# A fused patch-embedding, attention and expert kernel: attention as one stream of 128 steps, taken in pairs on TensorE

## The reference, cut to what matters

```python
h = tok_ref(x, W, b, cls_token, pos_enc)         # 32 images, 36 patches + 1 class token, 256 wide
h = concatenate([h, txt], axis=1)                # + 77 text tokens: T = 114 tokens an image
h = h + attn_ref(layernorm(h), Wq, Wk, Wv, Wo)   # 16 heads of 64, causal softmax, + its own input
h = h + ffn_ref(layernorm(h), ...)               # 8 experts, top 2, capacity 570, exact gelu
# attn_ref: q, k, v = x @ Wq, x @ Wk, x @ Wv
#   scores = q k^T / 8 + causal mask;  out = softmax(scores) v;  x + out @ Wo
```

## Time and profile before

| | us |
|---|---|
| median of 3 runs | 954.19 (951.41 to 954.93) |
| the profiled execution | 953.52 |
| its span, first to last instruction | 951.6 |
| first score matmul / last output projection's end | 51.8 / 679 |
| busy: PE, PEld | 869.6 (91%), 754.2 (79%) |
| busy: DVE, ACT, POOL | 556.2 (58%), 516.0 (54%), 370.5 (39%) |
| mean granted clock of TensorE | 0.96 |

### The profile page before, as it was taken

One profiled execution on the slowest core, in us unless ns is written; L12 is line 12 of the kernel. 1 busy time (PEld: TensorE's weight loads), 2 busy tenths in 40 slices (PEclk: granted clock), 3 DMA queues, 4 the chain that ended last, 5 costly groups with the idle time before them and its releaser, 6 DMA issues.

```text
span 951.6 us, 19817 instructions
## 1 busy us (share of the span) xinstructions
PE 869.6 (91%) x6897; PEld 754.2 (79%) x6897; DVE 556.2 (58%) x2433; ACT 516.0 (54%) x1686; POOL 370.5 (39%) x677
## 2 busy tenths in 40 slices
PE   4898999999999999999999999997708999999996
PEld 4676787797788778779777877875708999999996
DVE  3566347528645753863775485476236767777761
ACT  3368438807824961880684386186016555565551
POOL 2134225345425424543542653554430333322333
PEclk8799899999999999999999999998758999999999
DMA  8224302012002101200200200100135655444322
GB/s 252 50 58 132 98 13 60 2 41 74 1 8 65 43 1 42 71 2 22 68 16 1 59 9 2 38 2 1 24 100 179 158 117 134 102 121 121 83 26 25
DMA packets 61908, 57.64 MB, mean 61 GB/s; under 512 B 26784, under 2 KB 56652, under 8 KB 61697
## 3 DMA queue, kind: packets, MB, share of 16 engines
q1 hardware_dynamic: 41170, 45.15, 15.5%
q0 software_dynamic: 18944, 9.76, 6.5%
q10 hardware_dynamic: 1696, 1.49, 0.6%
HBM read 34.25 MB, written 21.89 MB: 59 GB/s over the span
## 4 chain that ended last, share of the span: by engine, by line
PE 82%; DVE 4%; POOL 4%; issue 4%; ACT 3%; DMA 1%; SPq 1%; POOLq 0%; DVEq 0%; ACTq 0%
PE bank L380 14%; PE bank L382 13%; PE bank L381 13%; PE pT_bank L1241 6%; PE score_bank L1232 6%; PE o_bank L1252 6%; PE score_bank L1130 4%; POOL pr L573 2%; PE o_bank L381 2%; PE o_bank L382 2%; PE o_bank L380 2%; PE score_bank L380 2%; PE score_bank L381 2%; PE score_bank L382 2%; ACT pr L706 2%
## 5 line engine op out<-in xcount | busy, mean ns | idle before, releaser
L573 POOL TENSOR_SCALAR pr<-pr,rc 114x114 f32<-114x114 f32 x512 | 179.7, 371 | 233.7 <-DVE rc L991 233.7
L706 ACT ACTIVATE pr<-sm,nb 114x114 f32<-114x114 f32 x512 | 192.1, 379 | 22.6 <-DVE nb L987 21.2
L983 DVE CUSTOM_DVE_ANT_0 sm<-score_bank,mask 114x114 f32<-114x114 f32 x512 | 110.5, 272 | 55.2 <-PE score_bank L1232 55.2
L604 POOL DMA_INDIRECT out_dram<-yout,dest x40 | 74.0, 1849 | 163.0 <-ACT yout L758 161.5
L554 POOL DMA_INDIRECT slots_dram<-rows,slot x64 | 72.8, 1137 | 128.2 <-DVE slot L950 93.3
L624 ACT ACTIVATE kT<-bank 128x456 f32<-128x456 f32 x64 | 34.1, 532 | 146.8 <-PE bank L382 146.8
L380 PE MATMUL bank<-xT_hi,wqkv_hi 128*128 128x456 f32 x256 | 103.5, 404 | 0.0
L1232 PEld LDWEIGHTS score_bank<-kT,qT 64*114 64x114 f32 x1024 | 62.1, 177 | 45.5 <-issue 35.3
L706 ACT ACTIVATION_READ_ACCUMULATOR pr<-sm,nb 114x1 f32 x512 | 97.0, 189 | 0.0
L381 PE MATMUL bank<-xT_lo,wqkv_hi 128*128 128x456 f32 x256 | 94.3, 368 | 0.0
L382 PE MATMUL bank<-xT_hi,wqkv_lo 128*128 128x456 f32 x256 | 94.3, 368 | 0.0
(11 more groups left out here) (198 smaller groups left out, 2228.1 us busy)
## 6 DMA issues: line engine op xcount, KB each, us to landing
stage_a<-in_L_ffn_w_dram SPq DMA_DIRECT2D x8, 1024.0 KB, 5.0
stage_b<-in_L_ffn_w_dram SPq DMA_DIRECT2D x8, 1024.0 KB, 7.1
slots_dram<-fill SPq DMA_DIRECT2D x8, 605.6 KB
xs<-slots_dram SPq DMA_DIRECT2D x8, 605.6 KB
pix<-in_x_dram SPq DMA_DIRECT2D x96, 36.0 KB, 2.3
hraw<-in_txt_dram SPq DMA_DIRECT2D x8, 308.0 KB
out_dram<-h SPq DMA_DIRECT2D x8, 308.0 KB
pix<-pix SPq DMA_DIRECT2D x7, 216.0 KB, 2.6
```

Source lines behind the costliest of these rows:

```text
L573: p = pool.tensor_scalar(pr[:, m % 4, i, :], pr[:, m % 4, i, :], rc[:, m % 4, i:i + 1], 1.0, ALU.mult, ALU.mult)
L604: pool.indirect_dma_start(out, bass.IndirectOffsetOnAxis(ap=dest[e % 2][:, t:t + 1], axis=0), yout[:, t, :], None, compute_op=ALU.add).the ...
L706: a = act.activation(pr[:, n % 4, i, :], sm[:, n % 2, i, :], ACT.Exp, bias=nb[:, n % 2, i:i + 1], scale=SCALE, accum_out=rs[:, n % 4, i:i ...
L983: m = dve.tensor_tensor_reduce(sm[:, n % 2, i, :], score_bank[i % 2][0:T, i // 2 * T:(i // 2 + 1) * T], mask[:, :], 1.0, NEG, ALU.add, ALU ...
```

## The change

1. The groups' loops become one loop over N = 0 to 132 (`steps()`: 128 steps and five that drain), g and n = divmod(N, 16). Nothing drains at a group's end.
2. On TensorE an even step issues `scores` of N and N + 1, then `weigh_values` of N - 5 and N - 4. Each step issues its own transposes, of N - 3 (`LAG_T` = 3, `LAG_O` = 5). `score_bank` now holds both steps, in other columns. VectorE masks N and N + 1 in the even step, the reciprocal and the low half between them.
3. The output projection of group g - 1 stands in steps 4 and 5 of group g (`AT_O`); the embedding in step 9 in one of the three banks instead of `score_bank[0]`; the second halves of the values in steps 5 to 8 of their own group; the first halves in steps 14, 15 and 0.
4. `pack` moves from step 10 to step 4 (`AT_PACK`), the addition into hx to steps 1 and 2, into two buffers. Dispatches go one by one into steps 4 to 11 of two groups later; other small parts get other steps.
5. The prologue makes four value projections instead of eight, and K, Q, K instead of Q, K, Q.

```diff
+        LAG_T, LAG_O = 3, 5
+        AT_O, AT_V2, AT_E, AT_M, AT_Y, AT_L, AT_X = 4, 5, 6, 9, 10, 11, 13
+        AT_PACK, AT_RSTD1, AT_RSTD2 = 4, 10, 8
+        STATS2, MOMENTS2, NORM2 = {6: (0, 1), 7: (2, 3)}, 7, {9: (0, 1, 2, 3)}
+        STATS1, MOMENTS1, NORM1 = {8: (0, 1), 9: (2, 3)}, 9, {11: (0, 1), 12: (2, 3)}
+        AT_DISPATCH = 4
+        def chunk_at(g, n):
+            name, c = ("Q", (n + 2) // 2) if n % 2 == 0 else ("K", (n + 3) // 2)
+            return (name, HP * g + c) if HP * g + c < HP * G else None
+        def value_jobs(g, n):
+            if n == 0 and g > 0:
+                return [(g, 3)]
+            if g + 1 < G:
+                return {14: [(g + 1, 0)], 15: [(g + 1, 1), (g + 1, 2)]}.get(n, [])
+            return []
...
 # TensorE
-                m = pe.matmul(score_bank[h][0:T, b * T:(b + 1) * T], qT[head, c % 2, tokens], kT[head, c % 2, tokens], start=True, stop=True)
+                m = pe.matmul(score_bank[h][0:T, tokens], qT[head, c % 2, tokens], kT[head, c % 2, tokens], start=True, stop=True)
+            for N, g, n in steps():
+                if n == AT_X and g + 1 < G:
+                    transpose_tokens("X", g + 1, xn, xn_done)
+                if n % 2 == 0:
+                    for m in (N, N + 1):
+                        if m < STEPS:
+                            scores(m)
+                    for m in (N - LAG_O, N - LAG_O + 1):
+                        if 0 <= m < STEPS:
+                            weigh_values(m)
+                if LAG_T <= N < STEPS + LAG_T:
+                    transpose_probs(N - LAG_T)
+                if g < G:
+                    if chunk_at(g, n):
+                        project(*chunk_at(g, n))
+                    for f, b in value_jobs(g, n):
+                        project_v(f, b, 0)
+                    if n - AT_V2 in range(GB):
+                        project_v(g, n - AT_V2, 1)
+                    if n == AT_E and g + 1 < G:
+                        transpose_patches(g + 1)
+                    if n == AT_M and g + 2 < G:
+                        embed(g + 2)
+                    if g > 0:
...
+                        if n - AT_O in range(2):
+                            project_o(g - 1, n - AT_O)
 # VectorE, in a step N
+                if N < STEPS and N % 2 == 0:
+                    mask_scores(N)
+                if 1 <= N <= STEPS:
+                    dve.wait_ge(exp_done, N)
+                    dve.reciprocal(rc[:, (N - 1) % 4, :], rs[:, (N - 1) % 4, :]).then_inc(recip_done, 1)
+                if N >= LAG_O:
+                    give_low_outputs(N - LAG_O)
+                if N < STEPS and N % 2 == 0:
+                    mask_scores(N + 1)
 # ScalarE, in a step N
+                if N >= LAG_O:
+                    take_outputs(N - LAG_O)
+                if LAG_T <= N < STEPS + LAG_T:
+                    m = N - LAG_T
+                    act.wait_ge(pT_done, m + 1)
+                    act.activation(pT[:, m % 2, :, :], ...).then_inc(pT_copied, 1)
+                if N < STEPS:
...
+                if g + 2 < G and n == AT_PACK:
+                    pack(g + 2)
 # GpSimd, in a step N
+                if g < G and n in (1, 2):
+                    if n == 1:
+                        pool.wait_ge(xn_done, GB * (g + 1))
...
+                    pool.tensor_tensor(hx[g % 2][:, b, :], hraw[:, b, :], xn[:, b, :], ALU.add).then_inc(hx_done, 1)
+                if 1 < g < G and n - AT_DISPATCH in range(TOPK * GB):
+                    dispatch(g - 2, n - AT_DISPATCH)
 # SP
+            for g in range(G):
+                if g + 1 < G:
                     sp.wait_ge(hx_done, 2 * g + 2)
                     load_text(g + 1)
+                if g + 2 < G:
                     sp.wait_ge(packed, g + 2)
                     load_pixels(g + 2)
```

More of the change, by code:

```diff
@@ L296, in count @@
+        JOB_AT = {job[:2]: i for i, job in enumerate(JOBS)}
         def count(jobs, engine=None):
             return sum(1 for j in jobs if engine is None or engine in j[2])
[L299 to L343, removed]
@@ L369, in ebank_free, with steps @@
             return [{"H": (gelu_done, NF * f + n + 1), "S": (xs_done, NX * f + n + 1), "Y": (y_done, CT * f + n + 1)}[was]]
-        def pair(g, n):
-            return g * PAIRS + n
+        STEPS = PAIRS * G
+        def steps():
+            for N in range(STEPS + LAG_O):
+                yield (N,) + divmod(N, PAIRS)
         def wait_all(eng, waits):
@@ L596, in _ @@
+            for i in range(TOPK * GB):
+                dispatch(G - 2, i)
             rstd(G - 1, vareps2, rstd2_done, ve2, rstd2)
@@ L1039, in _ @@
-            body(0, first=True)
-            for g in range(1, G - 2):
-                body(g)
-            body(G - 2)
-            body(G - 1, last=True)
-            jobs = Jobs("end")
+                            drain_e(g + 1, i)
+                    if n == AT_M + 1 and g + 2 < G:
+                        drain_embedded(g + 2)
+                    if g > 0:
+                        if n == AT_Y + 1:
+                            drain_y(g - 1)
+                        if n == AT_L + 1:
+                            route(g - 1, 0)
+                        if n - 1 - AT_O in range(2):
+                            drain_o(g - 1, n - 1 - AT_O)
@@ L1308, in body @@
-                if not last and not (isinstance(g, int) and g == G - 2):
-                    embed(g + 2)
-                if not first:
-                    count_places(jobs, g - 1)
-                if first:
-                    pe.wait_ge(wo_lo_done, 1)
-                pe.wait_ge(o_lo, pair(g, PAIRS))
-                for k in range(2):
-                    project_o(jobs, k)
-                if not last:
-                    project(jobs, "Q", 0)
-                    project(jobs, "K", 0)
-                    project(jobs, "Q", 1)
@@ L1322, in _ @@
[L1322 to L1332 removed]
+                            logits(g - 1)
+                        if n - AT_O in range(2):
+                            project_o(g - 1, n - AT_O)
@@ L1335, in e_claim @@
+                if n == AT_C and g > 1:
+                    count_places(g - 2)
+            for i in range(2):
+                project_o(G - 1, i)
+            transpose_tokens("Y", G - 1, rows[(G - 1) % 2], xn2_done)
+            logits(G - 1)
+            count_places(G - 1)
             def e_claim(name, e, k):
```

700 lines of the change are left out of this document (302 added, 398 removed).

## The result

The changed kernel takes **928.86 us** (median of 4 runs, 927.24 to 930.4), the kernel before 952.8 in the same comparison (951.38 to 954.93): a ratio of 0.9745, 95 % interval 0.9723 to 0.9766. The forecast was 921.8, with a range of 905 to 946. The profiled execution took 927.2 (span 925.3), so it is 5.4 over the forecast's own sum, which was made against a profiled execution too.

What follows compares the result with a forecast made beforehand. TensorE bounds the groups, through changes of the used array's shape, then seams. From the profiled 953.5 us, 34.1 less for pairs, 6.0 less for one stream and 8.4 more for the pixels make 921.8 us; range 905 to 946.

Steps and rivals of the forecast that it cites:

- What bounds the kernel: TensorE in the groups: mainly changes of the used array's shape, then 19.3 us of waits, nearly all near group seams.
- Rival 3: TensorE's gaps belong to each block's first operands, pairs bring them back: 955.9 us, no change; chance 0.06.
- Part 1: Scores and weighings issued for two steps at once on TensorE: 27 fewer shape changes a group, -34.1 us.
- Parts 1 and 2: Group loop: pairing two steps' scores and weighings, -34.1 us; one stream instead of draining and refilling groups, -6.0 us.
- part 3: Pixel packing moved to step 4: group 0's weighing in step 6 waits, +8.4 us once; hidden in steady groups.
- Step 13's size: TensorE's wait in step 13, 0.6 plus about 1.3 beyond its transposes: 1.9 us in each of seven groups, 13.3.
- One for one: Group 0's clock: the new wait brings a low-clock stretch, the one after the old 2.11 us idle goes: 0.
- Rival 2: The clock falls at step 13 of each group, 7 x 3.3 = 23 us: 945 us; chance 0.15.
- First scores: Start of the loop: four value projections leave the prologue, so scores start 5.6 us earlier; net nothing.
- Rival 4: ScalarE takes over in the pairs: slower than before from 5.87 us a pair, 966 at 6.0; chance 0.08.

Runs made afterwards that it cites:

- kernel without pairs: Changed kernel, still one stream, but each step issues its own scores and its own weighing and VectorE masks in each step: 944.78 us (0.9919).
- single weighings: Changed kernel with paired scores, but each step weighs its own values: 938.43 us (0.9843).
- single scores: Changed kernel with paired weighings, but each step does its own scores: 945.12 us (0.9915).
- one more change: Changed kernel with an even step's transposes put between the two steps' scores and the two steps' weighing: 943.43 us (0.99).

## Why the prediction was right, and where its steps were off

- **What bounds the kernel.** Changes of shape: shown. Five orders of the same matmuls give nearly the same price for each change, one of them with the very same blocks. Rival 3 (the gap belongs to the operands) is refuted. Of the seams the waits of rows 4 are gone; what that alone was worth was not measured.
- **Part 1's price.** A plain pair was to take 5.30 and takes 5.34, which is what three changes at the prediction's 0.153 make of 5.80 (5.47 where the counting of places adds two small matmuls). 27 changes a group at 0.158 were to save 4.27 of TensorE's time; its busy time fell by 78.16 - 74.12 = 4.04.
- **Parts 1 and 2, which owns what.** This step was wrong. The sum of the two was -40.1; the spans fell by 26.3, and with part 3's 8.5 that makes some 35. Their shares are further off. By the prediction the pairs gave 34.1, of which 3 changes a group (3.8) come with the one stream anyway: 30.3. The kernel without pairs shows 16.8 for them (by spans), and 951.6 - 942.1 = 9.5 for the stream with its wait for the pixels, where the prediction had 6.0 + 3.8 - 8.4 = 1.4. The waits of step 13, 13.3 in the sum, were booked on the stream. Most of them come only with the pairs, because pairs leave step 13 without scores and weighing: by the columns 1.32 a group, 9.2 in seven. That 30.3 - 13.3 = 17.0 is close to the 16.8 is partly luck: beside the 9.2, the pairs lose 0.37 a group at the seam and some of group 0 and of the clock, and the kernel without them loses 0.7 a group for the maximum and 1.0 by its start. How the stream's own share splits was not measured.
- **Step 13's size.** 1.9 was laid out (0.6 for xn, 1.3 for xT). In group 2 the transposes take 1.25 to the next block where eight spacings of 0.10 make 0.8, so 0.45 for xn; and the K projection starts 255.56 - 253.29 = 2.27 after the probabilities' transposes, which need 0.39: 1.9 for xT. Together 2.3. What was missed is the query copy: the prediction let the K projection wait for xT_lo alone, but it waits for the drains before it too. The kernel with that copy first shows it: there the wait for xT is 254.59 - 252.85 - 0.39 = 1.35, the size that was laid out.
- **At the seam** a wait of 0.37 for oT_lo is left in the first weighings of step 4. It was in no term.
- **Part 3.** The best term. Predicted: the pixels' packing 11.8 us behind the addition, TensorE at the weighing at 62.1, released from 70.5. Measured: 67.93 - 55.54 = 12.4, the first of the two weighings at 61.79, the second at 70.88, a wait of 8.5 against 8.4. Hidden in the other groups, as said. Taking it away gave 9.8.
- **Clock.** One for one was nearly so in group 0: a stretch of 10.2 us at 0.50, half of it idle, for one of 6.8. Rival 2 came in part: stretches of 3.4 us at 0.50 in groups 3 and 5, which make these groups 1.6 longer, and none in groups 0, 1, 2, 4 and 6, which have the same wait in step 13. The rule that the prediction took from the Trainium skill (TensorE: Matmul & The Clock Gate, Part 4: PE-mode transpose, transposes don't count as busy in the same way) was to lower the clock at step 13 of every group; here it doesn't. Whether transposes count less is not settled by that. The wait alone does not tell where the clock falls: it fell behind waits of 0.41 and 1.04 (single weighings, two groups of seven) and not behind one of 1.39 (single scores, none). The whole stretch from the first token transpose to the K projection orders the cases better. In the changed kernel it is nothing but transposes and waits for 3.5 us, and the clock fell in two groups of seven (three with packing in step 7); with one more change 3.7 us, and three groups; with the query copy first 3.0 to 3.2 us, and none. With single weighings it is 3.9 us with eight weighings in it, and two groups; with single scores 3.3 to 3.5 us with eight scores in it, and none. So the transposes, twelve at 0.10 us in each, may have their part in it; no run varied them alone.
- **First scores** at 45.73 (said: 46.2), and a steady group of 76.03 (said: 75.2, where the prediction's own terms, 80.57 - 4.27 - 6.0/7, give 75.4).
- **Rival 4** (ScalarE takes over) needed pairs of 5.87; they take 5.34.

The 5.4 us between sum and profile, by stretches: from the first scores to the last token transposes of group 7 the time fell by (684.52 - 51.8) - (656.38 - 45.73) = 22.1, where the sum has 26.1; 3.1 of the 4.0 are the two stretches at the lower clock. That the rest is so small is luck too: the 0.4 by which step 13's waits are longer and the 0.37 at the seam, seven times each, make another 5.4, so that other terms gave some 4.5 more than the sum has, and which ones was not traced. The start gave 6.1, not 5.6. Behind the groups it is 1.8 longer (925.3 - 656.38 against 951.6 - 684.52), where the sum has nothing: 1.2 of it in the experts, which start with 8.1 us at 0.50 instead of 5.1. The first row of the experts in the kernel before and after:

```profile
716.74 1.78 PE L1345 MATMUL bank<-ident,xs 114*128 114x114 f32 x8 [20.90 <-DMA xs<-slots_dram]
...
689.20 1.78 PE L1273 MATMUL bank<-ident,xs 114*128 114x114 f32 x8 [21.23 <-DMA xs<-slots_dram]
```

The clock returned to 1.00 at 721.8 and at 697.3. What decides the length of such a stretch was not tried.

## What to carry to other kernels

Where TensorE is the bound, count the places where the used shape of the array changes, price one from starts in the trace, and group blocks of equal shape: it paid 0.48 us per pair of steps here. Grouping takes small blocks away from where they stood as cover, though, so look behind each place that they leave; here the waits of one step took a third of the gain in a steady group, and other work moved into that place, with the operands' makers one step earlier, brought back as much (a steady group of 75.5 became one of 74.1). Of a first group in a pipeline, lay out the loads by themselves: it has less work to hide them.

## What was not expected of the hardware

- A change of shape costs nearly the same wherever it stands: 0.15 to 0.21 us in five orders of the same matmuls, between 64x114, 114x64 and 114x114 or 128x128 blocks, and nothing between the last two. The Trainium skill (TensorEngine Tiling (Array Packing), Key Properties) says that changing the tiling mode drains TensorE; the traces agree in that these changes cost time; whether it is a drain they don't show.
- The same wait of 1.72 us behind the same blocks was followed by a granted clock of 0.50 in two groups of seven and not in the other five (in three of seven with the packing in step 7); one of 1.18 was followed by it in none, one of 1.39 behind scores in none, and one of 1.04 behind a weighing, with 0.41 before it, in two.
